# Letting GpSimd's gathers follow TensorE's count of feed-forward steps in a graph layer with a ternary feed-forward

## The reference

```python
def gnn(x, src, dst, W_self, b_self, W_neigh, gamma, beta, alpha):
    deg = segment_sum(ones_like(src), dst, 6250)
    neigh = segment_sum(x[src], dst, 6250) / maximum(deg, 1.0)[:, None]
    h = x @ W_self + b_self + neigh @ W_neigh
    h = layernorm(h) * gamma + beta
    return where(h >= 0, h, alpha * h) + x

def ffn(x, w_gate, w_up, w_down):              # weights ternary by groups of 128
    return bitlinear(silu(bitlinear(x, w_gate)) * bitlinear(x, w_up), w_down)

x = x + gnn(layernorm(x), src, dst, ...)
x = x + ffn(layernorm(x), ...)
```

## Time and profile before

| | |
|---|---|
| runs | 1811.42, 1826.8, 1832.73 us; median 1826.8 us |
| profiled execution | 1812.78 us, its span 1811.0 us |
| mean granted TensorE clock | 0.931 of full speed |
| busy share | TensorE 84%, ScalarE 65%, VectorE 58%, GpSimd 54% |
| gathers | 882, with 231 MB of the 354 MB that all DMAs moved |

### The profile page before, as it was taken

The page is one execution under the profiler, slowest core; times in us unless marked ns, Lnnn a source line. Parts: engine busy times, 40 slices in busy tenths (PEclk is TensorE's granted clock), DMA queues, the critical chain, the costliest instruction groups (busy, mean ns, idle before and its releaser), DMA issues.

```text
span 1811.0 us, 22718 instructions
## 1 busy us (share of the span) xinstructions
PE 1515.5 (84%) x6819; PEld 625.7 (35%) x6820; DVE 1058.9 (58%) x2254; ACT 1182.7 (65%) x2250; POOL 969.2 (54%) x944
## 2 busy tenths in 40 slices
PE   7999978967888889879797898788876877877897
PEld 3454423433332333323233333233332232332343
DVE  8888526544555665554664555547465455473866
ACT  5477300146676777858786686677775876877886
POOL 1623366655556656556675665566656547665000
PEclk9999999987998999989998999899998988998999
DMA  9779488975767777667676777576667657776101
GB/s 284 254 231 273 143 308 272 284 229 151 207 175 222 200 193 219 189 188 216 194 210 184 225 205 197 161 224 190 191 174 211 182 173 200 202 193 173 39 9 40
DMA packets 199788, 353.88 MB, mean 195 GB/s; under 512 B 92380, under 2 KB 94144, under 8 KB 199666
## 3 DMA queue, kind: packets, MB, share of 16 engines
q0 software_dynamic: 70560, 231.27, 44.7%
q1 hardware_dynamic: 129106, 121.15, 22.3%
HBM read 295.79 MB, written 39.62 MB: 185 GB/s over the span
## 4 chain that ended last, share of the span: by engine, by line
PE 62%; issue 12%; ACT 10%; DVE 5%; another core or an unknown queue 4%; DMA 3%; SPq 2%; DVEq 0%; ACTq 0%
PE f_ps L1088 18%; PE f_ps L1089 17%; PE f_ps L879 14%; PE agg_ps L987 10%; ACT f_ps L1183 6%; DMA x1T<-hsx 2%; PE side_ps L1030 1%; ACT acc L1193 1%; ACT hT L1208 1%; DVE acc L1531 1%; DVE nmr L1278 1%; DMA edges<-dst_pad 1%; PE agg_ps L875 1%; DMA node_table<-work 1%
## 5 line engine op out<-in xcount | busy, mean ns | idle before, releaser
L832 POOL DMA_INDIRECT rows<-node_table,idx x882 | 899.9, 1020 | 566.9 <-issue 257.9
L1183 ACT ACTIVATE f_ps<-f_ps,ratio 128x512 f32<-128x512 f32 (+2 forms) x1305 | 773.8, 658 | 344.1 <-PE f_ps L1089 166.6
L1088 PE MATMUL f_ps<-x1T,tern 128*128 128x512 f16 (+2 forms) x1144 | 431.5, 381 | 157.7 <-DMA x1T<-hsx 43.1
L1089 PE MATMUL f_ps<-x1T,tern 128*128 128x512 f16 (+2 forms) x1144 | 429.1, 379 | 3.0 <-issue 3.0
L987 PE MATMUL agg_ps<-rows,hot 128*64 128x512 f16 x2058 | 286.6, 416 | 15.1 <-issue 13.3
L1531 DVE SCALAR_TENSOR_TENSOR acc<-f_ps,scl,acc 128x512 f32<-128x512 f32 (+2 forms) x143 | 102.2, 716 | 297.7 <-PE f_ps L1089 177.8
L1088 PE MATMUL f_ps<-hT,tern 128*128 128x512 f16 (+2 forms) x572 | 220.9, 388 | 50.0 <-issue 23.7
L1088 PEld LDWEIGHTS f_ps<-x1T,tern 128*128 128x128 f16 x1144 | 113.4, 99 | 405.3 <-issue 174.6
L1089 PE MATMUL f_ps<-hT,tern 128*128 128x512 f16 (+2 forms) x572 | 219.3, 386 | 2.1 <-issue 2.1
L987 PEld LDWEIGHTS agg_ps<-rows,hot 128*64 128x64 f16 x2058 | 125.9, 119 | 178.8 <-issue 105.6
L1089 PEld LDWEIGHTS f_ps<-x1T,tern 128*128 128x128 f16 x1144 | 114.5, 100 | 93.1 <-issue 23.2
(11 more groups left out here) (186 smaller groups left out, 1616.7 us busy)
## 6 DMA issues: line engine op xcount, KB each, us to landing
rows<-node_table,idx POOLq DMA_INDIRECT x882
hsx<-own_rows SPq DMA_DIRECT2D x49, 256.0 KB
hsx<-in_x SPq DMA_DIRECT2D x48, 256.0 KB
out_nodes<-work SPq DMA_DIRECT2D x48, 256.0 KB, 2.2
node_table<-work SPq DMA_DIRECT2D x30, 256.0 KB, 4.9
xj<-xnt_rows SPq DMA_DIRECT2D x26, 256.0 KB
acc<-own_rows SPq DMA_DIRECT2D x23, 256.0 KB
own_rows<-acc SPq DMA_DIRECT2D x23, 256.0 KB
```

The source lines that it names most:

```text
L832: pool.indirect_dma_start(out=rows[:, at, :], out_offset=None, in_=table[:, :], in_offset=bass.IndirectOffsetOnAxis(ap=of, axis=0)).then_i ...
L1088: pe.matmul(to, lhs, parts[0], start=g == 0, stop=False, skip_group_check=True)
L1089: pe.matmul(to, lhs, parts[1], start=False, stop=True, skip_group_check=True).then_inc(p_ff, 1)
L1183: act.activation(ps, ps, ACT.Copy, scale=ratio[:, w if up else 2, j:j + 1]).then_inc(a_scaled, 1)
```

## The change

Each gather now also waits for TensorE's count of feed-forward steps. The gather at place n of the whole list (18 per block) waits until all steps that `AT` puts ahead of tick n - 9 are done: one gather a tick, and nine ticks ahead of the slot in which its block is summed. Nothing else is changed.

```diff
     SLOT_OF = {s: t for (t, k), steps in AT.items() for s in steps}
+    step_at = [at for at, steps in AT.items() for s in steps]
...
+    LEAD = 9
+
+    def steps_before(t, k):
+        return sum(at < (t, k) for at in step_at)
...
                 for j in ORDER:
                     after(pool, p_used, freed_by(b, j))
+
+                    after(pool, p_ff, steps_before(*divmod(max(b * STEPS + ORDER.index(j) - LEAD, 0), STEPS)))
                     gather(row_at(b, j), idx[:, b % 4, j:j + 1], gathered[len(BURST_ROUNDS) * (b % 2) + FIRST_USE[j]])
```

## The result

The changed kernel takes 1729.9 us, median of 3 runs (1729.33 to 1733.91), against 1826.8 us (1811.42 to 1832.73): a ratio of 0.955, 95% interval 0.950 to 0.960. The profiled execution took 1729.3 us, 83 us less than that of before. Throughout, ratios and their intervals leave out executions that took over 1.5% longer than the fastest of their kernel, while the medians are over all.

What follows compares the result with a forecast made beforehand. TensorE was taken as the bound, held back by long unbroken gather runs, with chunk starts as second limit. Shorter delays -24 us and late sums +2 us gave -22 us: 1826.8 to 1805 us, range 1773 to 1829 us.

Steps and rivals of the forecast that it cites:

- hold-ups: Places beside long unbroken gather runs where TensorE's results are there or nearly so, but its semaphores arrive late.
- the chain's unknown share: Part of the chain that ended last named "another core or an unknown queue": 4%, some 72 us, forecast to become 3%.
- The hold-up in slot 33: Late TensorE counts beside ten gathers; TensorE stood 4.45 us, and the delay was to end 1.0 to 3.5 us earlier.
- a third: 24 us less: Gain from shorter delays of TensorE's counts, taken between 0 and three quarters of the chain's 72 us.
- Is the new wait ever the last one?: Step asking where the count stops GpSimd: only when caught up during a burst and, above all, when counts are late.
- the 1.0 us tick: Ticks 0 to 8 of slot 32 took 1.0 us each, too short for GpSimd to keep up with one gather a tick.
- The wait itself: Cost of another semaphore on 780 gathers: even 39 us would lie in GpSimd's 566.9 us idle time, so 0.
- Late sums: Bursts waiting for later gathered rows, at burst 1 of slots 10, 38 and 46: 3.8 us each at worst, 2 us taken.
- Chunk starts: Waits for transposed rows, 39.1 us in 8: same traffic in short slots, so 0, at most a few tenths each.
- (a): Rival: the late counts vanish because pauses fall inside gather runs; all 72 us go, 1755 us; chance 0.12.
- (b): Rival: nothing changes, as the count is never the last wait or gathers are not the cause; 1827 us; chance 0.28.
- (c): Rival: slower, late counts move and grow between burst 0 and burst 1, costing 57 us; 1862 us; chance 0.15.

Runs made afterwards that it cites:

- e11: Kernel before with each gather replaced by a GpSimd fill of its row buffer with zeros: 1515.2 us against 1828.3, ratio 0.827.
- e7: Kernel before plus the new wait on only a block's first nine gathers, on a chip with late counts: 1901.4 us against 1809.6, ratio 1.04 from one execution.
- e9: Kernel before with gathers moving 256 bytes a row in place of 2048, no new wait: 1815.6 us against 1809.6, ratio 1.006.
- e8: Kernel before plus the new wait on only a block's last nine gathers: 1793.6 us against 1809.6, ratio 0.983.
- e10: Kernel before with a tiny GpSimd fill behind each gather, no new wait: 1839.1 us against 1809.6, ratio 1.016.
- e1: Kernel before plus the new wait on only a block's first nine gathers, on the chip without late counts: 1566.7 us against 1560.4, ratio 1.004.

## Why the prediction was wrong

**The mechanism held in the main.** The new wait acts on the hold-ups, through the late count, and it shortens them and doesn't end them. GpSimd's waits carry the feed-forward matmul's name, and the chain's unknown share is at 3%, both as forecast. ScalarE's remote waits were to fall by a third; they fell to less than half. The hold-up in slot 33 was to end 1.0 to 3.5 us earlier; TensorE stood for 3.2 us less. (The 3.5 us took the seventh gather to start at 1214.6, although the count that it waits for came through only at about 1216.0; by that it was 2.1 us at most.) One part did not hold: that TensorE is held until the last gather has landed. Behind the last gather's end nothing is late for more than 2.6 us, but more than half of the late rescalings (75 of 137) start while gathers are still being issued; the two places of the earlier trace rows were of the other half.

**The step that failed is the size: "Between these ends, 0 and three quarters of the chain's 72 us, I take a third: 24 us less."** The base was wrong. The chain of waits gives "unknown" only those pieces at which it could find no releaser. Three quarters of the gain lie elsewhere: this share fell by some 20 of 83 us. What a late count costs beyond it can be seen in part: the steps that start late in a row behind it (the chain's "issue" fell by some 60 us); the clock, which is at its lower level for 252 us before, 188 after and 102 on the chip without hold-ups, with TensorE's busy time for the same matmuls at 1515.5, 1493.0 and 1426.1 us (the bursts 0 alone lost 18 us, mostly so); and the slots before the ninth, 18 us. What hold-ups cost as a whole is shown by e11 on one of these chips, 313 us less with the gathers gone, and by the chip that has none, on which the kernel before takes some 267 us less. Those two differ from the kernel before in more than the hold-ups, so they are rough. A third of 267 us is 89 us, beside the 97 measured; since the sum of lags fell by 46% and not by a third, that the two agree so well is partly luck. The lower bound of the forecast's own range also leaves out the 2 us of costs (1775, not 1773), which changes no more than 2 us.

**"Is the new wait ever the last one?"** was half wrong. I argued from the 1.0 us tick that the count would brake only in bursts and in hold-ups. It was the last wait 215 times: a hold-up of a few us makes GpSimd stop for 2 to 3 us, and that breaks the very run that goes with it. From slot 9 on all runs but one had 8, 10 or 18 gathers before (68 runs); now 69 of 111 have seven or fewer. The mean lag at the sixth gather of a run went from 5.1 us to 2.3 (14 steps). "The gathers held back are not spared: they come behind the hold-up" was the reason for staying near the lower end. It is right as such, and e7 shows how dear it is, 4% or more, where the second nine places have no brake. With the brake on all places what comes behind is broken up as well.

**The costs** were small, as forecast. The wait itself: GpSimd's idle time fell from 566.9 to 486.5 us and nothing waits for it but the bursts. Late sums: in slots 10, 38, 42 and 46 burst 1 was 5 us or so late, at most 5.9 us of waiting for rows, and behind that wait it ran at 1.2 GHz (4.5 us in place of 2.3, granted clock 0.50 to 0.55). From the start of burst 0 to the next step these slots took 13.4, 15.0, 13.4 and 10.5 us before and 13.1, 12.0, 12.5 and 12.6 us after: slot 46 lost 2.1 us and the others nothing, so my 2 us was right in size, though there were four such waits of about 5 us and not three of 3.8, and what covered them elsewhere may be the hold-ups that became shorter. Chunk starts: the waits for the transposed rows went from 39.1 us in 8 to 17.2 in 5; I had put 0, and 22 us is a part of the gain that I can't divide, since one wait more or less there is 4 to 8 us.

**The rivals.** (a) priced the end of the hold-ups at 72 us, on the same wrong base: the change keeps half of them and yet wins 97 us. (b) is refuted: the count is the last wait 215 times, and e11 shows that without gathers there is no hold-up. The rule of the Trainium skill beside it ("SBUF — State Buffer", "Who interferes with whom", that DMA never contends with a compute engine) is neither confirmed nor refuted for the ports: e9, with a third of the bytes a second, agrees that bytes hold nothing back. But read as "gathers cost TensorE nothing" it would have been wrong by 17% on a chip with hold-ups (e11); on the one without them no run took the gathers out. (c) went the other way: the stretch from burst 0 to burst 1, with the gathers moved to it, took 409 us in place of 424. What I had as (c)'s mechanism, hold-ups that move and grow, does exist in e7, where the second nine places go without the brake, and in the stretch from burst 0 to burst 1 in e8 (492 us in place of 424).

## What to carry to other kernels

The share of "unknown" in the chain of waits is a lower end for what a late signal costs, not its size: before pricing a stall, take its presumed cause out as a whole (here the fills of e11) and read the whole from that. Breaking up the runs works, by a brake that reacts to the late signal or by a plain rest of about 1.5 us, but on all places of the queue: on the first half of them alone the brake collected work that then came in one piece, and the kernel was slower than without it. And ask whether the thing that is being repaired is there on every chip: here one of the four chips of the experiments has none of it, and on that one the halves of the repair cost up to 1.2%. The whole repair was not run there.

## What the runs showed of the hardware

- With the same program, ScalarE's rescalings started within 0.04 us of the end of TensorE's step on one chip, and up to 10 us after it in the trace of before (15 us in e10); all 137 late ones of that trace stand beside a run of gathers or within 2.6 us of its end. The kernel took 1560 us and 1803 to 1846 us.
- In runs of 8 and 10 the lag is there from the third gather on, at a mean spacing of 1.33 us; in runs of 18 mostly from the tenth. It doesn't depend on the bytes (2048 or 256 a row), and it isn't there when GpSimd is busy with fills of 0.9 us.
- Late counts come in a lot (239 within 0.06 us of the one before) or 1.4 us apart (96), where a step otherwise takes 0.43 us.
- With a rest of 1.54 us behind four gathers it was nearly gone (sum of lags 40 us against 606), with one of 0.82 us it wasn't (525 us).
- A gather's own transfers were about as fast on either kind of chip: taking the packets in order, 80 a gather, the last ended 3.5 us after its start before and 3.7 us in e1 (medians), so the hold-up isn't a slower DMA.
- Open: by what way issued gathers delay TensorE's counts, whether its work or only its signals are late, what sets the onset in a run, and why one chip is free of it.
